# Slice tokens: the normalising on GpSimd, the low token product a tile later, TensorE's waits gathered

## The reference, cut to what matters

```python
xn = _layernorm(x)                                  # 6250 x 256
x_mid = (xn @ W_x + b_x)                            # 8 heads of 64
slice_weights = softmax((x_mid @ W_slice + b_slice) / temp, axis=-1)   # per node and head, 64 slices
slice_norm = slice_weights.sum(axis=nodes)
slice_token = einsum('bhnc,bhng->bhgc', fx_mid, slice_weights) / (slice_norm + 1e-5)
```

## Time and profile before

| | |
|---|---|
| median of 3 runs | 2148.08 us |
| the profiled execution | 2157.28 us |
| its span | 2155.5 us |
| mean granted TensorE clock | 0.96 |
| TensorE busy (matmul) | 1887.3 us, 88% |
| VectorE busy | 1511.3 us, 70% |
| ScalarE busy | 1336.4 us, 62% |
| GpSimd busy | 1449.1 us, 67% |

### The profile page before, as it was taken

How to read it: one execution, slowest core, us unless ns; L and a number is a source line. 1 busy time by engine, 2 the same in 40 slices (tenths; PEclk the granted TensorE clock), 3 DMA queues, 4 the chain that set the end, 5 groups by cost and what they waited for, 6 DMA issues and landing times. The chain is left out here.

```text
span 2155.5 us, 38774 instructions
## 1 busy us (share of the span) xinstructions
PE 1887.3 (88%) x10100; PEld 1558.8 (72%) x10100; DVE 1511.3 (70%) x3467; ACT 1336.4 (62%) x2400; POOL 1449.1 (67%) x989
## 2 busy tenths in 40 slices
PE   4979999999989988998899889988993696888888
PEld 2757888787777777777777777777773574677778
DVE  6946877776777667767777676667672587777756
ACT  3637777776676667766766676667662365666623
POOL 2216888888888888888888888888888560455500
PEclk9999999999999999999999999999997697999979
DMA  9878889888988898889888888898886980000002
GB/s 346 341 273 162 160 156 175 163 154 154 174 151 145 155 173 150 150 153 176 157 142 154 178 155 144 150 175 150 153 135 92 324 265 12 11 0 0 2 29 101
DMA packets 288980, 325.43 MB, mean 151 GB/s; under 512 B 30118, under 2 KB 251721, under 8 KB 288688
## 3 DMA queue, kind: packets, MB, share of 16 engines
q0 software_dynamic: 112896, 102.81, 38.8%
q1 hardware_dynamic: 172576, 217.21, 31.8%
q10 hardware_dynamic: 3280, 2.83, 0.4%
HBM read 167.64 MB, written 154.97 MB: 150 GB/s over the span
## 5 line engine op out<-in xcount | busy, mean ns | idle before, releaser
L930 POOL DMA_INDIRECT sums<-summed,out_idx x784 | 1243.4, 1586 | 297.6 <-issue 208.8
L984 PE MATMUL bank<-wf,hidT 128*128 128x256 f32 x3136 | 798.9, 383 | 0.0
L984 PEld LDWEIGHTS bank<-wf,hidT 128*128 128x128 f32 x3136 | 545.9, 192 | 52.9
L1075 ACT ACTIVATE hidT<-bank,bf 128x512 f32<-128x512 f32 x392 | 269.8, 688 | 262.5 <-PE bank L962 258.2
L1170 DVE TENSOR_TENSOR msg_low<-msg,msg_high 128x512 fp32r<-128x512 f32 x392 | 272.0, 694 | 171.1 <-ACT msg_high L1095 171.1
L1201 DVE TENSOR_TENSOR msg<-bank,gathered 128x512 f32<-128x512 f32 x392 | 269.3, 687 | 111.1 <-PE bank L984 104.7
L1095 ACT ACTIVATE msg_high<-msg 128x512 fp32r<-128x512 f32 x392 | 247.4, 631 | 96.7 <-DVE msg L1201 93.5
L982 PE MATMUL bank<-gnn_bf_halves,ones 128*128 128x256 f32 x784 | 297.2, 379 | 0.0
L1083 ACT ACTIVATE summed<-pair 128x516 f32<-128x516 f32 x392 | 230.4, 588 | 79.6 <-DMA sums<-summed,out_idx 78.7
L1102 ACT ACTIVATE gathered<-bank 128x512 f32<-128x512 f32 x392 | 231.8, 591 | 37.0 <-PE bank L972 36.7
L972 PE MATMUL bank<-window,spread 128*128 128x256 f32 x784 | 194.2, 329 | 63.7 <-DVE spread L1165 43.0
(11 more groups left out here) (330 smaller groups left out, 2741.7 us busy)
## 6 DMA issues: line engine op xcount, KB each, us to landing
window<-xn_halves SPq DMA_DIRECT2D x392, 128.0 KB, 4.1
sums<-gate SPq DMA_DIRECT2D x32, 800.0 KB, 9.7
id_row<-id_rows SPq DMA_DIRECT2D x98, 256.0 KB
attr<-attr_rows SPq DMA_DIRECT2D x98, 256.0 KB, 4.6
xn_halves<-xn_halves SPq DMA_DIRECT2D x7, 1792.0 KB, 6.6
id_row<-id_rows SPq DMA_DIRECT2D x98, 128.0 KB, 3.4
sums<-summed,out_idx POOLq DMA_INDIRECT x784
res<-sums SPq DMA_DIRECT2D x24, 512.0 KB, 7.6
```

The costliest lines, as they stand in the source:

```text
L930: nc.gpsimd.indirect_dma_start(g.sums_dram[k], bass.IndirectOffsetOnAxis(ap=out_idx[:, ET * c + t:ET * c + t + 1], axis=0), summed[c % 2][ ...
L984: mm = T.matmul(out, hidT[:, j // 2, f, ds((2 * (j % 2) + t) * P, P)], g.wf2[:, f, :], start=False, stop=f == CB - 1)
L1075: A.activation(hidT[:, h, f, :], hps[:], ACT.Silu, bias=g.bf1[:, f:f + 1]).then_inc(hid_ready, 1)
```

## The change

- `normalise` moves from ScalarE (an activation with scale and bias) to GpSimd (a tensor_scalar, multiply and add, with the same two columns). In its step t GpSimd normalises tile t+2 and then makes the low halves of tile t-1. Its loop is written out over all 49 tiles.
- `tokens` is split: tokens_high (the 8 products with wh) stays at its place, for tile t-2; tokens_low (the 4 products with wl) comes in the next step, right behind the next logits.
- TensorE waits at two places in a step: for w_low ahead of the logits, and, in weights_in, for w_ready, wT_ready, x_low and w_high ahead of turn_w. turn_x and the logits keep their own.
- x2h gets 4 buffers instead of 2, and the buffers are guarded by high_made, tok_made and w_low on ScalarE and GpSimd.

The order of TensorE's step t becomes: logits(t), tokens_low(t-3), turn_w(t-2), turn_x(t+1), tokens_high(t-2).

```diff
--- before.py
+++ after.py
@@ -1705,11 +1705,11 @@
     w_ready = sem("h_w_ready")
     w_turned = sem("h_w_turned")
     wT_ready = sem("h_wT_ready")
-    tok_made = sem("h_tok_made")
+    tok_made, high_made = sem("h_tok_made"), sem("h_high_made")
     x_high, x_low = sem("h_x_high"), sem("h_x_low")
     w_high, w_low = sem("h_w_high"), sem("h_w_low")
     x2 = [sb(f"x2_{p}", [P, C], F32) for p in range(RING)]
-    x2h = [sb(f"x2h_{p}", [P, C], F32R) for p in range(2)]
+    x2h = [sb(f"x2h_{p}", [P, C], F32R) for p in range(RING)]
     x2l = [sb(f"x2l_{p}", [P, C], F32R) for p in range(2)]
     xTh = [sb(f"xTh_{p}", [P, CB, P], F32R) for p in range(2)]
     xTl = [sb(f"xTl_{p}", [P, CB, P], F32R) for p in range(2)]
@@ -1773,42 +1773,59 @@
                 mm.then_inc(logit_made, 1)
 
             def turn_w(t, r):
+                for q in range(HGB):
+                    mm = nc.tensor.transpose(wps[:, ds(q * P, P)], ex[r][:, ds(q * P, P)], g.ident[:])
+                mm.then_inc(w_turned, 1)
+
+            def tokens_high(t, r):
+
+                rows = rows_of(t)
+                for y in (x2h[r], x2l[r % 2]):
+                    for q in range(HGB):
+                        mm = nc.tensor.matmul(acc[q], wh[r % 2][0:rows, ds(q * P, P)], y[0:rows, :],
+                                              start=is_before(t, 1) and y is x2h[r] and q % 2 == 0,
+                                              stop=False, skip_group_check=True)
+                mm.then_inc(high_made, 1)
+
+            def tokens_low(t, r):
+
+                rows = rows_of(t)
+                for q in range(HGB):
+                    mm = nc.tensor.matmul(acc[q], wl[r % 2][0:rows, ds(q * P, P)], x2h[r][0:rows, :], start=False,
+                                          stop=is_known(t, NT - 1) and q % 2 == 1, skip_group_check=True)
+                mm.then_inc(tok_made, 1)
+
+            def weights_in(t):
                 pe.wait_ge(w_ready, t + 1)
                 if not is_before(t, 1):
                     pe.wait_ge(wT_ready, t)
-                for q in range(HGB):
-                    mm = nc.tensor.transpose(wps[:, ds(q * P, P)], ex[r][:, ds(q * P, P)], g.ident[:])
-                mm.then_inc(w_turned, 1)
-
-            def tokens(t, r):
-
-                rows = rows_of(t)
                 pe.wait_ge(x_low, t + 1)
                 pe.wait_ge(w_high, 2 * t + 2)
-                for x, y in ((wh, x2h), (wh, x2l), (wl, x2h)):
-                    if x is wl:
-                        pe.wait_ge(w_low, 2 * t + 2)
-                    for q in range(HGB):
-                        mm = nc.tensor.matmul(acc[q], x[r % 2][0:rows, ds(q * P, P)], y[r % 2][0:rows, :],
-                                              start=is_before(t, 1) and x is wh and y is x2h and q % 2 == 0,
-                                              stop=is_known(t, NT - 1) and x is wl and q % 2 == 1,
-                                              skip_group_check=True)
-                mm.then_inc(tok_made, 1)
 
             def step(t, r):
+                if not is_before(t, LAG + 1):
+                    pe.wait_ge(w_low, 2 * (t - LAG))
                 logits(t, r)
+                if not is_before(t, LAG + 1):
+                    tokens_low(t - LAG - 1, (r - LAG - 1) % RING)
                 if not is_before(t, LAG):
+                    weights_in(t - LAG)
                     turn_w(t - LAG, (r - LAG) % RING)
                 if exists(t + 1):
                     turn_x(t + 1, (r + 1) % RING)
                 if not is_before(t, LAG):
-                    tokens(t - LAG, (r - LAG) % RING)
+                    tokens_high(t - LAG, (r - LAG) % RING)
 
             turn_x(0, 0)
             over_tiles(pe, step)
             for t in range(NT - LAG, NT):
+                pe.wait_ge(w_low, 2 * t)
+                tokens_low(t - 1, (t - 1) % RING)
+                weights_in(t)
                 turn_w(t, t % RING)
-                tokens(t, t % RING)
+                tokens_high(t, t % RING)
+            pe.wait_ge(w_low, 2 * NT)
+            tokens_low(NT - 1, (NT - 1) % RING)
 
         @block.scalar
         def _(act):
@@ -1821,12 +1838,6 @@
             def expo(t, r):
                 act.wait_ge(shifted, t + 1)
                 A.activation(lps[r][:], lps[r][:], ACT.Exp).then_inc(exp_ready, 1)
-
-            def normalise(t, r):
-                if not is_before(t, RING):
-                    act.wait_ge(x_low, t - RING + 1)
-                A.activation(x2[r][:], g.res[:, t, :], ACT.Identity, bias=m.mean[:, ds(t, 1)],
-                             scale=m.rstd[:, ds(t, 1)]).then_inc(x2_ready, 1)
 
             def copy_w(t):
                 act.wait_ge(w_turned, t + 1)
@@ -1836,10 +1847,13 @@
             def round_both(t, r):
 
                 act.wait_ge(x2_ready, t + 1)
-                if is_known(t, NT - 1):
-                    act.wait_ge(tok_made, t - 1)
-                A.activation(x2h[r % 2][:], x2[r][:], ACT.Copy).then_inc(x_high, 1)
+                if not is_before(t, RING):
+                    act.wait_ge(tok_made, t - RING + 1)
+                A.activation(x2h[r][:], x2[r][:], ACT.Copy).then_inc(x_high, 1)
                 act.wait_ge(w_ready, t + 1)
+                if not is_before(t, 2):
+                    act.wait_ge(high_made, t - 1)
+                    act.wait_ge(w_low, 2 * t - 2)
                 for k in range(2):
                     cols = ds(k * HG // 2, HG // 2)
                     A.activation(wh[r % 2][:, cols], ex[r][:, cols], ACT.Copy).then_inc(w_high, 1)
@@ -1852,11 +1866,7 @@
                 expo(t, r)
                 if not is_before(t, 1):
                     round_both(t - 1, (r - 1) % RING)
-                if exists(t + 2):
-                    normalise(t + 2, (r + 2) % RING)
-
-            normalise(0, 0)
-            normalise(1, 1)
+
             copy_xT(0, 0)
             over_tiles(act, step)
             round_both(NT - 1, (NT - 1) % RING)
@@ -1869,18 +1879,34 @@
 
             def low_halves(t, r):
                 pool.wait_ge(x_high, t + 1)
-                G.tensor_tensor(x2l[r % 2][:], x2[r][:], x2h[r % 2][:].bitcast(F32), ALU.subtract).then_inc(x_low, 1)
+                if not is_before(t, 2):
+                    pool.wait_ge(high_made, t - 1)
+                G.tensor_tensor(x2l[r % 2][:], x2[r][:], x2h[r][:].bitcast(F32), ALU.subtract).then_inc(x_low, 1)
+                if not is_before(t, 2):
+                    pool.wait_ge(tok_made, t - 1)
                 for k in range(2):
                     cols = ds(k * HG // 2, HG // 2)
                     pool.wait_ge(w_high, 2 * t + k + 1)
                     G.tensor_tensor(wl[r % 2][:, cols], ex[r][:, cols], wh[r % 2][:, cols].bitcast(F32),
                                     ALU.subtract).then_inc(w_low, 1)
 
+            def normalise(t, r):
+                if not is_before(t, RING):
+                    pool.wait_ge(x_low, t - RING + 1)
+                    pool.wait_ge(turned, t - RING + 1)
+                G.tensor_scalar(x2[r][:], g.res[:, t, :], m.rstd[:, ds(t, 1)], m.mean[:, ds(t, 1)], ALU.mult,
+                                ALU.add).then_inc(x2_ready, 1)
+
             def step(t, r):
+                if exists(t + 2):
+                    normalise(t + 2, (r + 2) % RING)
                 if not is_before(t, 1):
                     low_halves(t - 1, (r - 1) % RING)
 
-            over_tiles(pool, step)
+            normalise(0, 0)
+            normalise(1, 1)
+            for t in range(NT):
+                step(t, t % RING)
             low_halves(NT - 1, (NT - 1) % RING)
 
         @block.vector
```

## The result

The changed kernel takes 2169.49 us (median of 4 runs, 2167.36 to 2174.48) against 2150.62 us for the kernel before (4 runs, 2145.38 to 2153.44). The ratio is 1.0092, with an interval of 1.0065 to 1.0118: **slower by 0.9%, some 19 us**. The direction and the mechanism were as forecast. The size was not: +12.2 us were forecast, and the time lies 1.5 us above the range. (The prediction names 2169.5 us for its profiled execution; that the measured median is the same number is chance.)

What follows compares the result with a forecast made beforehand. A circle of waits through several engines, 4.18 us a tile, was taken as the bound. A new link adds 0.27 in 46 tiles, 12.4; with +0.1 - 0.3 that is +12.2 us on 2148.08: 2160.3, range 2149 to 2168.

Steps and rivals of the forecast that it cites:

- part 2: TensorE's waits ahead of turn_w: new link ex, wh, turn_w, wT, xTh, 2.02 for 1.75; period 4.18 to 4.45 us.
- the prediction's own sign of being off in size: At wh on ScalarE: the size is off if wh starts later than 0.03 us behind ex's end.
- rival B: At turn_w's load on TensorE: same circle, load follows wh after 0.06; period 4.39, +9.5 us, 2157.6; 25%.
- upper bound: At wh on ScalarE: two added waits cost 0.06 each at worst; period 4.57, a rise of 18 us.
- part 3: Low products between logits and turn_w on TensorE: done 2.34 after xTl starts, wh at 2.74, hidden with 0.40 to spare.
- rival A: Ahead of turn_w, wh isn't last; circle xTl, logits, tokens_low, turn_w, wT, xTh: period 3.88, saving 14 us, 2134; 7%.
- part 4: GpSimd's new normalise: 0.7 us taken (0.26 to 1.4; 0.4 by the skill), hidden while under 2.3.
- part 5: The stage's ends: first normalise +0.1 us, sooner last logits -0.3; GpSimd's written-out loop and more x2h buffers nothing.
- rival D: TensorE's clock falls to 1.2 GHz as the engine idles more: up to +148 us, 2296; 2%.

Runs made afterwards that it cites:

- e2: The changed kernel with only TensorE's waits for x_low and w_high moved back to ahead of the high token products: 2146.72 us, ratio 0.9973.
- e3: The kernel before with only TensorE's waits for x_low and w_high moved ahead of turn_w: 2164.5 us, ratio 1.0062.
- e4: The changed kernel with ScalarE's loop over tiles written out, its three waits at wh kept as they are: 2160.04 us, ratio 1.0041.
- e9: The changed kernel with ScalarE's waits for high_made and w_low moved from in front of wh to ahead of x2h: 2171.95 us, ratio 1.0077.
- e5: The changed kernel with the x_low and w_high waits back at the high products and ScalarE's loop written out: 2145.3 us, ratio 0.9983.
- e10: The changed kernel with x_low and w_high waits at the high products, low products behind turn_x, ScalarE's loop written out: 2127.73 us, ratio 0.9887.
- e8: The changed kernel with two more small tensor_scalar operations on GpSimd in front of each normalise from tile 2 on: 2172.28 us, ratio 1.0103.
- e1: The changed kernel with ScalarE's waits for high_made and w_low put before the wait for ex, making that the last: 2164.6 us, ratio 1.0065.

## Why the prediction was wrong

- **Mechanism and direction: right.** The circle through wh, turn_w and wT was named with its links, and the sum of the links is the period in the trace. e2 and e3 show it from both sides.
- **The step that failed: part 2's terms for ScalarE's two pick-ups.** ex to wh was kept at 0.72 ("both are long satisfied, and I price them at zero"), and wh's end to wT was put at 0.81. In the loop they are 0.81 and 0.84. In detail, wh starts 0.12 behind ex's end and not 0.03 (+0.09, the prediction's own sign of being off in size), wT starts 0.13 behind turn_w's end and not 0.04 (+0.09), and TensorE's load follows wh after 0.05 and not 0.11 (-0.06, rival B's short wake-up, right by itself): 4.45 + 0.09 + 0.09 - 0.06 = 4.57. So the new link costs 0.40 in the loop and not 0.27; over the 46 tiles, those written out included, it is 17.6 us for 12.4. The 0.81 came from the stage's tail and the second wait's zero from TensorE; the loop's ScalarE is neither. That the upper bound was 4.57 too is luck: it stood for two more waits at wh, 0.06 each, and nothing at wT.
- **Why that loss:** e4 and e9 show that it belongs to the separate instruction that stands in the loop between such a wait and the work. It is in front of wh only by the change's two added waits, and at wT it costs only because turn_w is now late. e5 and e10 take it from wT and gain 0.09 and 0.08, as expected.
- **The low product, a tile later** (part 3): hidden as forecast. By the rows above it is through 0.53 + 1.48 + 0.47 = 2.48 after xTl's start, and wh after 2.83: 0.35 to spare for the 0.40 forecast, and turn_w's load still waits 0.44 for wh behind it. The remark that without this cover it would be rival A's circle held: e2 is that circle, with 4.11 for 3.88. It was short by wT's late pick-up (0.12 for 0.04), and by logits that start and run slower where they start right behind xTl (0.53 + 1.48 for 0.47 + 1.40, by 1926.77, 1927.30 and 1928.78 in the profile after).
- **GpSimd** (part 4): 0.56, between the 0.7 taken and the 0.4 estimated beside it; nobody waits for it. Right, and tested by e8.
- **The ends** (part 5): xTl of tile 2 came 11.30 us after the first normalise for 11.34, and after the last xTl 10.21 us passed for 10.39; together -0.2, as forecast (+0.1 - 0.3).
- **The clock** (rival D): 1.00 in all windows of the stage, with TensorE busy 86%.
- **The number and the range.** The time came out 9.2 us above the 2160.3 predicted: 5.1 by the stage (17.3 for 12.2), 2.5 because the median used as the base was 2148.08 and the same kernel stood at 2150.62 with a fourth run, and 1.6 that the stage doesn't explain, within the scatter. The range doesn't follow from its own words: part 2's upper bound over the base is 2148.08 + 18 = 2166, not 2168, and 2149 is 8.6 below rival B's 2157.6, not 3 to 5.

## What to carry to other kernels

Before gathering an engine's waits in one place, look at each: a wait may move ahead of other work only if it ends no later than the waits already there, and here one that ended some 0.4 us after TensorE was ready closed a circle through three engines (VectorE, ScalarE, TensorE). In a stage where no engine is full, add up the links of the circle of waits, start to start; they give the period to a few hundredths, and show that a product of 0.47 us is free in one place on TensorE and costs 0.38 in another. Take each link's price from rows of the same engine in the same loop, not from the steps written out at its ends. And where an operation waits on the circle, see that no other instruction, a register's or a wait's, comes to stand between that wait and the operation.

## What the runs showed of the hardware

- On ScalarE an operation that has a register instruction between its releaser's end and itself starts 0.12 to 0.14 us after that end (wh and wT in the loop of the changed kernel, 40 tiles each); with a wait instruction alone in between it is 0.09 to 0.12 (e1), and with nothing in between 0.03 to 0.04 (e4, e9 for wh). Constants don't help by themselves: e4's three waits, with the one for ex first, cost nothing, and e1's, with it last, cost 0.10 to 0.12 in the written-out steps.
- On TensorE turn_w's load follows wh after 0.05 with nothing in between (1929.60 to 1929.65) and after 0.11 with a separate wait in between (1842.76 to 1842.87 in the profile after).
- GpSimd's tensor_scalar with two column scalars takes 0.56 us for 256 columns, 0.36 for 24 (e8).
